# A graph network kernel: the first norm and node table in parts, and node sums turned further ahead

## What is computed

```python
h = jnp.maximum(_layernorm(x, axis=-1), 0.0)
x = x + _L0_gnn_ref(h, edge_index, edge_attr_64, ...)   # h + segment_sum of a 3-layer softplus MLP of [h[r], edge_attr]
h = jnp.maximum(_layernorm(x, axis=-1), 0.0)
x = x + _L1_gnn_ref(h, ..., src, dst, edge_type_8, ...) # gated unit over sums of A[edge_type] @ h[src]
h = jnp.maximum(_layernorm(x, axis=-1), 0.0)
x = x + _L2_gnn_ref(h, src, dst, edge_attr_8, ...)      # tanh network over both ends and a basis of 8
h = jnp.maximum(_layernorm(x, axis=-1), 0.0)
x = x + _L3_gnn_ref(h, edge_index, ...)                 # two mean convolutions
```

## Time and profile before

| | |
|---|---|
| median of three runs | 10138.35 us |
| the profiled execution | 10130.24 us, of it 10128.6 us are the span of the trace |
| setup, first norm, node table | 0 to about 142 us |
| edge phase 0 | 142 to 1603 us |
| second boundary | 1603 to about 1779 us |
| edge phases 1 to 4 | 1779 us to the end |

### The profile page before, as it was taken

How to read it: one execution, slowest core, us unless ns; L and a number is a source line. 1 busy time by engine, 2 the same in 40 slices (tenths; PEclk the granted TensorE clock), 3 DMA queues, 4 the chain that set the end, 5 groups by cost and what they waited for, 6 DMA issues and landing times.

```text
span 10128.6 us, 209066 instructions
## 1 busy us (share of the span) xinstructions
PE 5756.1 (57%) x32026; PEld 3578.1 (35%) x32026; DVE 4352.4 (43%) x12092; ACT 2451.7 (24%) x4667; POOL 6779.5 (67%) x7783
## 2 busy tenths in 40 slices
PE   6999998244444447999999972444444422222222
PEld 4777774122222223444444432333333211121111
DVE  6888886232323235777777761111111111111111
ACT  5999995000000002333333320000000000000000
POOL 3333331777777775777777757777777677777777
PEclk9999999555555558999999985555555555555555
DMA  3333333111111112222222221111111111111111
GB/s 109 96 96 97 96 97 131 27 31 30 31 30 30 30 31 50 61 62 61 61 61 60 61 42 28 29 28 29 29 29 29 26 28 29 29 29 29 29 29 28
DMA packets 563973, 489.90 MB, mean 48 GB/s; under 512 B 307755, under 2 KB 361840, under 8 KB 563824
## 3 DMA queue, kind: packets, MB, share of 16 engines
q0 software_dynamic: 215488, 230.46, 12.7%
q1 hardware_dynamic: 315952, 255.93, 8.9%
q10 hardware_dynamic: 32448, 2.65, 0.2%
HBM read 427.12 MB, written 62.00 MB: 48 GB/s over the span
## 4 chain that ended last, share of the span: by engine, by line
POOL 35%; PE 32%; issue 16%; DVE 7%; ACTq 5%; DMA 3%; ACT 1%; POOLq 1%; DVEq 1%; SPq 0%
POOL mov L741 33%; PE ps L1695 6%; PE ps L1520 5%; PE ps L1546 4%; ACTq L392 4%; PE ps L1553 3%; PE ps L1687 3%; POOL outs L741 2%; PE ps L1714 1%; DVE scr L1011 1%; PE ps L1680 1%; PE ps L1676 1%; PE ps L1544 1%; DMA mov<-tab_msg,idx 1%; PE ps L1705 1%
## 5 line engine op out<-in xcount | busy, mean ns | idle before, releaser
L1520 PE MATMUL ps<-outs,mov 128*64 128x64 f32 x9984 | 1371.1, 319 | 3882.6 <-DMA mov<-tab_q,idx 1429.5
L1520 PEld LDWEIGHTS ps<-outs,mov 128*64 128x64 f32 x9984 | 1158.4, 221 | 4204.3 <-issue 4202.9
L911 DVE TENSOR_TENSOR acc<-acc,ps 64x64 f32 (+1 forms) x1664 | 352.8, 212 | 4259.2 <-PE ps L1520 4085.9
L741 POOL DMA_INDIRECT outs<-tab_u,idx x1664 | 1583.9, 952 | 580.6 <-issue 479.1
L741 POOL DMA_INDIRECT mov<-tab_h,idx x1612 | 1528.7, 948 | 559.6 <-issue 469.6
L741 POOL DMA_INDIRECT mov<-tab_msg,idx x1612 | 1538.1, 954 | 518.2 <-issue 463.2
L741 POOL DMA_INDIRECT mov<-tab_q,idx x1612 | 1527.0, 947 | 528.1 <-issue 490.9
L1011 DVE TENSOR_TENSOR scr<-ps,scr 128x512 f32<-128x512 f32 x1664 | 1063.9, 686 | 361.4 <-PE ps L1687 334.2
L1695 PE MATMUL ps<-scr,w_bas 128*64 128x512 f32 x3328 | 898.6, 618 | 0.0
L705 POOL TENSOR_TENSOR scr<-outs 128x128 f32<-128x128 f32 x416 | 191.7, 461 | 814.0 <-DVE outs L921 813.2
L921 DVE TENSOR_TENSOR outs<-rel,iota_w 128x256 f32<-128x256 f32 x1664 | 706.2, 425 | 42.4 <-issue 29.0
(11 more groups left out here) (230 smaller groups left out, 8440.4 us busy)
## 6 DMA issues: line engine op xcount, KB each, us to landing
mov<-in_dst_row SPq DMA_DIRECT2D x832, 128.0 KB, 2.7
mov<-in_ea_T SPq DMA_DIRECT2D x416, 128.0 KB, 2.5
mov<-tab_msg SPq DMA_DIRECT2D x3328, 0.2 KB
mov<-tab_msg ACTq DMA_DIRECT2D x3328, 0.2 KB
mov<-tab_h SPq DMA_DIRECT2D x3328, 0.2 KB
mov<-tab_h ACTq DMA_DIRECT2D x3328, 0.2 KB
mov<-tab_q SPq DMA_DIRECT2D x3328, 0.2 KB
mov<-tab_q ACTq DMA_DIRECT2D x3328, 0.2 KB
```

The lines of the kernel that those rows point to most:

```text
L741: nc.gpsimd.indirect_dma_start(out=gat(e, u)[:, k, :], out_offset=None, in_=table, in_offset=bass.IndirectOffsetOnAxis(ap=idx[:, u, k:k + ...
L911: nc.vector.tensor_tensor(into, into, bank(banks[u % len(banks)])[0:rows, 0:W], ALU.add) \
L1520: last = mm(bank(banks[u % len(banks)])[0:width, 0:W], values(u)[:, k, :], sel(e, u)[:, k, :], start=k == 0, stop=k == TL - 1)
```

## The change

- **Loads.** SP no longer loads `x`; ACT issues it in two transfers once the indices have landed (64 blocks, then 40), on its own queue.
- **Constants.** GpSimd makes the three that DVE's index work needs first, and DVE waits for these alone; `fold` waits for the rest.
- **First norm and table.** The norm goes by seven parts (six of 16 blocks, one of 8): DVE runs `centre`, `vary` and `finish` of a part, ACT `square` and `root`, two parts ahead. The mean is no longer scaled by an instruction of its own. PE transposes straight from `h` (no staging copy); the table's product uses four PSUM banks and four buffers of `outs`, and three of four groups are copied out by ACT, the fourth by DVE. PE's and ACT's loops are written out. `fold` is cut in two and moves to banks 6 and 7.
- **GpSimd.** Each clearing of `acc` is eight instructions, and the residual addition is seven, each after its part of the norm.
- **Windows.** In edge phases 0 and 1 DVE sets the windows before it waits for the stores.
- **Second boundary.** After `messages(0)` PE turns the sums 4, 5 and 6; after `messages(j)` the sums j + 6.

```diff
+PB = 16
...
+CLEARS = 8
...
+        PARTS = [(b, min(b + PB, NB)) for b in range(0, NB, PB)]
+        LOADED_AHEAD = -(-len(PARTS) // 2)
+        def copied_by_act(j):
+            return j // GB * (GB - 1) + j % GB + 1
...
-            sp.dma_start(x[:, :, :], t["x"].rearrange("(b p) c -> p b c", p=P128)).then_inc(x_loaded, 16)
...
-            store_groups("T0", [tab_g], H)
+            for j in range(NG):
+                if j % GB == GB - 1:
+                    sp.wait_ge(dve_copied, j // GB + 1)
+                else:
+                    sp.wait_ge(act_copied, copied_by_act(j))
+                sp.dma_start(tab_g[j * GN:(j + 1) * GN, :].rearrange("(k p) c -> p k c", p=P128),
+                             outs[:, j % GB, :].rearrange("p (k c) -> p k c", k=GB)).then_inc(stored[j % GB], 16)
             windows(0, slice(D, P128), tab_g, H, [(mov[0:D], t["ea64_T"])], used0)
...
+            assert made[0] == N_IOTAS
...
-            nc.gpsimd.memset(acc[:, :], 0.0).then_inc(cleared, 1)
+            for n in range(CLEARS):
+                nc.gpsimd.memset(acc[:, n * NP // CLEARS:(n + 1) * NP // CLEARS], 0.0).then_inc(cleared, 1)
...
-            pool.wait_ge(normed, 5)
-            nc.gpsimd.tensor_tensor(x[:, :, :], x[:, :, :], h[:, :, :], ALU.add).then_inc(residual, 1)
+            for q, (b0, b1) in enumerate(PARTS):
+                pool.wait_ge(first_normed, q + 1)
+                nc.gpsimd.tensor_tensor(x[:, b0:b1, :], x[:, b0:b1, :], h[:, b0:b1, :], ALU.add).then_inc(residual, 1)
...
-            nc.gpsimd.memset(acc[0:D, :], 0.0).then_inc(cleared, 1)
+            for n in range(CLEARS):
+                nc.gpsimd.memset(acc[0:D, n * NP // CLEARS:(n + 1) * NP // CLEARS], 0.0).then_inc(cleared, 1)
...
-            dve.wait_ge(consts, N_CONSTS)
+            dve.wait_ge(consts, N_IOTAS)
...
+            def fold_first():
+                dve.wait_ge(consts, N_CONSTS)
...
+            def centre(q):
+                b0, b1 = PARTS[q]
+                if q == 0:
+                    dve.wait_ge(x_ahead, 16)
+                if q == LOADED_AHEAD:
+                    dve.wait_ge(x_loaded, 16)
+                order(nc.vector.tensor_reduce(out=part_of(mean, q), in_=part_of(x, q), axis=AX.X, op=ALU.add))
+                nc.vector.scalar_tensor_tensor(out=part_of(h, q),
+                                               in0=part_of(mean, q).unsqueeze(2).to_broadcast([P128, b1 - b0, D]),
+                                               scalar=-1.0 / D, in1=part_of(x, q), op0=ALU.mult, op1=ALU.add) \
+                    .then_inc(first_centred, 1)
+            def vary(q):
+                dve.wait_ge(first_squared, q + 1)
+                nc.vector.tensor_reduce(out=part_of(rstd, q), in_=part_of(squares_nb, q), axis=AX.X, op=ALU.add) \
+                    .then_inc(first_varied, 1)
+            def finish(q):
+                b0, b1 = PARTS[q]
+                dve.wait_ge(first_rooted, q + 1)
+                order(nc.vector.reciprocal(part_of(rstd, q), part_of(rstd, q)))
+                nc.vector.scalar_tensor_tensor(out=part_of(h, q), in0=part_of(h, q), scalar=0.0,
+                                               in1=part_of(rstd, q).unsqueeze(2).to_broadcast([P128, b1 - b0, D]),
+                                               op0=ALU.max, op1=ALU.mult).then_inc(first_normed, 1)
+            def copy_rows(j):
+                dve.wait_ge(first_formed, j + 1)
+                if j >= GB:
+                    dve.wait_ge(stored[j % GB], 16 * (j // GB + 1))
+                nc.vector.tensor_copy(outs[:, j % GB, :], bank(2 + j % GB)).then_inc(dve_copied, 1)
...
-                    dve.wait_ge(cleared, e + 1)
-                    wait_stores(dve, AFTER[e])
+                    dve.wait_ge(cleared, CLEARS * (e + 1))
...
                     set_windows(e, p)
+                    if e < 2:
+                        wait_stores(dve, AFTER[e])
...
+            for q in range(min(2, len(PARTS))):
+                centre(q)
+            fold_first()
+            for q in range(len(PARTS)):
+                vary(q)
+                if q + 2 < len(PARTS):
+                    centre(q + 2)
+                if q >= 2:
+                    copy_rows((q - 2) * GB + GB - 1)
+                finish(q)
+                if q == 0:
+                    fold_second()
+            for q in range(max(0, len(PARTS) - 2), len(PARTS)):
+                if q * GB + GB - 1 < NG:
+                    copy_rows(q * GB + GB - 1)
             edge_phase(0, edge_mlp)
...
+            act.wait_ge(ints_loaded, 16 * len(INT_LOADS))
+            ahead = PARTS[LOADED_AHEAD - 1][1]
+            for name, first, last in ((x_ahead, 0, ahead), (x_loaded, ahead, NB))[:1 + (ahead < NB)]:
+                act.dma_start(x[:, first:last, :],
+                              t["x"][first * P128:last * P128, :].rearrange("(b p) c -> p b c", p=P128)).then_inc(name, 16)
+            act.preload_act_table_set("sqrt_and_others")
+            def square(q):
+                part = slice(*PARTS[q])
+                act.wait_ge(first_centred, q + 1)
+                nc.scalar.activation(squares_nb[:, part], h[:, part], ACT.Square).then_inc(first_squared, 1)
+            def root(q):
+                part = slice(*PARTS[q])
+                act.wait_ge(first_varied, q + 1)
+                nc.scalar.activation(rstd[:, part], rstd[:, part], ACT.Sqrt, scale=1.0 / D, bias=eps_c[:, 0:1]) \
+                    .then_inc(first_rooted, 1)
+            def lift_first(j):
+                act.wait_ge(first_turned, j + 1)
+                if j >= 2:
+                    act.wait_ge(first_formed, j - 1)
+                nc.scalar.activation(hT[0:D, j % 2, :], bank(j % 2)[0:D, :], ACT.Copy).then_inc(first_lifted, 1)
+            def copy_rows(j):
+                act.wait_ge(first_formed, j + 1)
+                if j >= GB:
+                    act.wait_ge(stored[j % GB], 16 * (j // GB + 1))
+                nc.scalar.activation(outs[:, j % GB, :], bank(2 + j % GB), ACT.Copy).then_inc(act_copied, 1)
+            act.wait_ge(consts, N_CONSTS)
+            for q in range(min(2, len(PARTS))):
+                square(q)
+            root(0)
+            act.wait_ge(bias_rt, 48)
+            for j in range(NG):
+                q, n = j // GB, j % GB
+                lift_first(j)
+                if n == 0 and q + 2 < len(PARTS):
+                    square(q + 2)
+                if n == 1 and q + 1 < len(PARTS):
+                    root(q + 1)
+                if j >= 1 and (j - 1) % GB != GB - 1:
+                    copy_rows(j - 1)
+            if NG % GB:
+                copy_rows(NG - 1)
...
+            def turn_first(j):
+                pe.wait_ge(first_normed, j // GB + 1)
+                if j >= 2:
+                    pe.wait_ge(first_lifted, j - 1)
+                for k in range(GB):
+                    last = nc.tensor.transpose(bank(j % 2)[0:D, k * P128:(k + 1) * P128], h[:, j * GB + k, :], ident[:, :])
+                last.then_inc(first_turned, 1)
+            def rows_g(j):
+                pe.wait_ge(first_lifted, j + 1)
+                if j >= GB and j % GB == GB - 1:
+                    pe.wait_ge(dve_copied, j // GB)
+                elif j >= GB:
+                    pe.wait_ge(act_copied, copied_by_act(j - GB))
+                for k in range(GB):
+                    last = mm(bank(2 + j % GB)[:, k * H:(k + 1) * H], hT[:, j % 2, k * P128:(k + 1) * P128], w_l0n[:, :],
+                              start=True, stop=True)
+                last.then_inc(first_formed, 1)
+            turn_first(0)
+            turn_first(1)
+            for j in range(NG):
+                rows_g(j)
+                if j + 2 < NG:
+                    turn_first(j + 2)
+            pe.wait_ge(fold_taken, 1)
...
                 messages(j)
-                if j + 4 < NG:
-                    turn_sums(j + 4)
+                for n in range(j + 6 if j else 4, min(j + 7, NG)):
+                    turn_sums(n)
                 if j + 2 < NG:
```

More of the change, by code:

```diff
@@ L220, in build_gnn @@
         windowed = sem("windowed")
-        normed = sem("normed")
         residual = sem("residual")
@@ L305, in done_of @@
             return g * n + it * (RING * n) + (u * n + step + 1 + RING * n - back)
-        LOOPS = ["T0", "T1"]
-        ADDS = {name: dict(T0=1, T1=0) for name in ("staged", "turned", "lifted", "formed", "settled")}
-        START = dict(settled=8)
-        STORES = dict(T0=(2, 1), T1=(4, 1))
-        def at(name, loop, grp, n=0, back=0):
-            before = START.get(name, 0) + sum(ADDS[name][k] * NG for k in LOOPS[:LOOPS.index(loop)])
-            return grp * ADDS[name][loop] + (before - back * ADDS[name][loop] + n + 1)
-        def end(name, loop):
-            return at(name, loop, NG - 1, ADDS[name][loop] - 1)
-        def stores_by(loop, buf):
-            total = 1
-            for k in LOOPS[:LOOPS.index(loop)] if loop else LOOPS:
-                if k in STORES and buf < STORES[k][0]:
```

(49 more changed lines are left out.)

120 lines of the change are left out of this document (39 added, 81 removed).

## The result

The changed kernel takes 10044.92 us (median of four runs, 10034.23 to 10046.54) against 10137.14 for the kernel before beside it: a ratio of 0.9906, 95% interval 0.9892 to 0.9919. Its profiled execution took 10034.23, of it 10032.6 are the span; before, 10128.6. The forecast was 10041, in a range of 10028 to 10076.

What follows compares the result with a forecast made beforehand. GpSimd, TensorE and issue share most of the wait chain; only setup (140 us) and second boundary (160 us) can move. Savings of 97.6 from 10130.2 give 10032.6; the median stands 8.1 higher: 10041 us, range 10028 to 10076.

Steps and rivals of the forecast that it cites:

- A: Setup: VectorE's index work can start with the last index load, at 11.6 instead of 16.84 us; 5.3 us saved.
- D: Window setting before the wait for the stores: 4.9 us saved at the first boundary, 5.0 (4 to 6) at the second.
- E: Second boundary, sums turned six ahead: TensorE sets the pace, 4.12 us a group; 48.8 us saved, bounds 38 to 51.
- F: Clearing of `acc` in pieces, at both boundaries: nothing saved; waits of 4.2 us a pair lie under the slack.
- B: Setup, norm until its first part is ready: 12.1 us instead of 38.6; 26.5 us saved, between 22 and 28.
- C: Table before phase 0: 1.75 us a group, 48.3 us instead of 55.4; 7.1 us saved, between 1 and 10.
- Port: First norm: GpSimd's additions hold each `centre` and `finish`, VectorE gains 13 us, table ends later; total 10054 us, chance 0.09.
- Clock: Phase 0: TensorE's lower clock level in more than 157 of 1461 us makes the kernel slower; chance 0.03.
- the bound on the loads of `x`: Setup: if all parameter loads were served before `x`, part 0 would be 6.6 us late; nothing was taken for it.

## Why the prediction was right, and where it was not

**Constants, six ahead, windows: right.** The sizes of A, D and E hold: 5.2, 5.5 and 5.2, 48.8. The two runs on six ahead and the one on windows show E and D apart; for A the releaser at 11.60 is the evidence. The 5.5 is good to about 1, as its step scatters by 1.8 between kernels that share it. In E two parts moved: 4.3 of the 48.8 belong to the pieces, since the last held instructions would have cost TensorE a wait. F called that nothing on the ground of slack in a pair, 12.4 against 7.05 and three pieces; that holds with the pieces, but the whole instruction's 7.75 doesn't fit, and the forecast never priced the change without them.

**Norm, B: 5.6 too optimistic.** The term that was mis-sized is the first half of `fold`: 2.2 taken, 4.5 as its upper bound, 6.7 measured (36.95 to 43.63, with the last copy). The bound let a cast be held for one piece, 1.4 each, as the pieces are 1.4 long. But pieces that are issued back to back act on a cast as one instruction, 5.21 to the end of all eight; taking the clearing away gave 0.21, a wait between the pieces 1.39. A row for a wider bound was there: in rows 5 L833, a tensor_scalar, lasted to the end of the clearing, though of a whole one. By the forecast's own count the cast began at 35.4 and the pieces ended at 41, so the hold could be 5.6 and not 1.4 a cast. The other 1.1 are index work that ended 1.3 late beside the constants (L779 1.67 and L780 0.77, both casts) and passes of 1.22 for 1.13, less a wait for ScalarE that was not there.

**Table, C: 10.7 too pessimistic.** 1.75 a group was taken and 1.33 measured, below the lower bound of 1.62: 25 x 0.42 = 10.5. That bound added busy times, half of 2.05 for the products and 0.60 for the transposes. Neighbours in TensorE's pipeline overlap in the trace: the transposes at 64.58 last 0.60, but the product starts at 65.02, 0.44 later. Rows 6 show the same, 98.70 to 99.17: 0.47 for a group of transposes whose busy time is 0.60. A pace is the difference of starts. TensorE set the pace, but with little to spare: in 59.70 to 65.02, four groups, it was busy all 5.32, VectorE 5.25 and ScalarE 4.80. No run takes the four banks, the missing staging copy or ScalarE's copies apart.

Both measured terms lie outside the bounds that the forecast gave them (B 20.9 against 22 to 28, C 17.8 against 1 to 10). The errors have opposite signs and cancel to 5.1, and the 7.5 lost in the untouched phases took that back: the closeness of the total is partly luck. The same holds for the median, which stood 10.7 above the profiled run and not 8.1.

**The rivals.** *Port* fell for the changed kernel: six additions of 2.35 and one of 1.27 held no pass of 16 blocks (1.22 to 1.24 throughout), as they start with a `vary`, and one of 8 blocks by 0.55, against the 2.2 a pass of the rival; TensorE waited for no norm in the table. But the mechanism is real and the margin thin. It appeared in three experiments as soon as the additions slipped from their places (3.35; 2.74, 2.50 and 2.51; 2.94), and a whole addition held the window instruction to 10.93. The Trainium skill ("SBUF — State Buffer", Who interferes with whom) says that an instruction of VectorE with two SBUF inputs contends with a GpSimd instruction that reads SBUF, not with one that only writes, and that casts and tensor_scalar contend in their two-port modes; the traces agree: the clearing held casts and tensor_scalar and no pass beside it (1.22 at 41.05 in the kernel with the cast ahead), the additions held passes and a tensor_scalar. By the same section whoever issues first has the shared pair for the whole instruction; of a run of instructions it says nothing. Here a run of pieces without a wait held the cast through all of them in the first boundary, while in the second three tensor_scalars got in after one piece each. What decides that was not found.

*Clock* was priced at x1.75 from rows 6, 3.58 against 2.05, as lower against upper level. But the granted clock reads 1.00 from 75 to 81, where the 3.58 lies, so that row is no price of the clock, and why those products were slow stays open. Message matmuls of the second boundary took up to 1220 ns at a granted 0.50 and 592 at 1.00. The forecast's 10041 took only the 1.0 and the 1.8 of the first group from such rows.

Of the bound on the loads of `x`, 6.6, a part came, 5.4 later than forecast, and lay within the room: the first pass waited for `passes_i` only. Whether `x` on SP's queue would do as well was not tried.

## What to carry over

Price a queue of an engine by differences of starts, not by sums of busy times. When long instructions are cut so that others get in, look at what is held and by how many pieces: for a cast a wait between them, or other work, made them let go here, cutting alone did not; for three tensor_scalars it did. An order in which two engines share a port works by phase: moving one side by a few us, even to make it faster, can cost what it gains, so follow each gain to the next mark before counting it.

## What was not expected of the hardware

- A 1x128 cast beside GpSimd's writes took 5.21 with eight pieces back to back, 4.93 with one long instruction, 1.39 with a wait between the pieces, 0.21 alone.
- GpSimd started the first addition of the program 6.72 to 8.48 after the end of a memset just before it (7.06, 7.14 and 8.48 in the three kernels in which part 0 had been ready for 5 us or more), and the reduction over the partitions 5.50 and 5.60 after one; later additions follow a memset at once. In the changed kernel both lie almost wholly in idle time (addition 0.73 after its norm). The Trainium skill ("GPSIMD Engine Reference", Instruction dispatch) gives about 6 us, without an instruction in the profile, for the first call to a kernel of GpSimd that has just been loaded; the sizes here are near that, but no run shows a load.
- Three small tensor_scalar instructions were held to 0.89, 1.41 and 1.42 (0.17 alone) by pieces 1.44 apart, while the tensor_scalars of one column at the first boundary took 0.13 to 0.15 beside the first piece.
